# Twelve x buffers instead of eight, statistics eight node blocks ahead, and a new order of VectorE's work in a node round

## What is computed

```python
h = maximum(layernorm(x, eps=1e-5), 0)            # (100000, 160)
s, v = h[:, :64], h[:, 64:].reshape(N, 32, 3)
w = relu(edge_feature @ W_fc1) @ W_fc2            # weights of each edge
tp = products(w, (s @ W_nl0)[dst], (v @ W_nl1)[dst], unit(edge_attr))
agg = segment_sum(tp, src, N) / 32
out_s = agg[:, :96] @ W_out_s + s @ W_skip0
out_v = agg_v @ W_out_v + v @ W_skip1
fs, gate = silu(out_s[:, :64]), sigmoid(out_s[:, 64:96])
return x + concatenate([fs, gate * out_v])
```

## Time and profile before

| | |
|---|---|
| Time, three runs | 1454.20, 1448.97, 1454.13 us; median 1454.13 |
| Profiled execution: span | 1322.7 us |
| Its own device time beside the span | not listed; the median less the span is 131.4 us |
| Busy share of TensorE, VectorE, ScalarE, GpSimd | 91%, 83%, 78%, 63% |
| Edge stages, node stage | about 0 to 610 us, 610 to 1323 us |
| From the residual of block 0 to that of block 97 | 631.52 to 1314.13 us |

### The profile page before, as it was taken

One profiled execution on the slowest core, in us unless ns is written; L12 is line 12 of the kernel. 1 busy time (PEld: TensorE's weight loads), 2 busy tenths in 40 slices (PEclk: granted clock), 3 DMA queues, 4 the chain that ended last, 5 costly groups with the idle time before them and its releaser, 6 DMA issues.

```text
span 1322.7 us, 33310 instructions
## 1 busy us (share of the span) xinstructions
PE 1197.9 (91%) x8853; PEld 998.1 (75%) x8853; DVE 1099.5 (83%) x4058; ACT 1029.0 (78%) x2446; POOL 828.6 (63%) x1077
## 2 busy tenths in 40 slices
PE   4899998999999999994999998999889999889986
PEld 2455557888888888883888787888778888778876
DVE  7999998888889888875688788888788888788775
ACT  2777776788878888864888788888888887888884
POOL 5555557787878888712766566566566666566651
PEclk9999997999999999996999999999999999999998
DMA  6000002344434443422888878888878888888873
GB/s 214 8 0 0 0 15 65 105 111 111 112 104 113 112 110 108 113 60 52 218 248 245 251 225 246 248 248 253 238 231 241 253 245 248 239 235 255 241 192 108
DMA packets 90930, 212.40 MB, mean 161 GB/s; under 512 B 15030, under 2 KB 56281, under 8 KB 90878
## 3 DMA queue, kind: packets, MB, share of 16 engines
q1 hardware_dynamic: 62462, 155.23, 35.4%
q0 software_dynamic: 28416, 56.56, 21.0%
HBM read 127.73 MB, written 84.00 MB: 160 GB/s over the span
## 4 chain that ended last, share of the span: by engine, by line
PE 38%; DVE 18%; ACT 9%; issue 9%; DMA 8%; POOL 2%; SPq 0%; DVEq 0%; ACTq 0%; POOLq 0%
DMA xb<-x 7%; PE bank L1419 6%; PE bank L1349 5%; DVE n_stat L858 5%; ACT nn L1178 4%; DVE ob L949 4%; PE bank L1289 4%; PE bank L1378 3%; PE bank L1366 3%; PE bank L1433 3%; PE bank L1362 3%; PE bank L1364 3%; PE bank L1334 2%; PE bank L1411 2%; DVE ob L956 2%
## 5 line engine op out<-in xcount | busy, mean ns | idle before, releaser
L574 POOL DMA_INDIRECT mg<-messages,slot_m x392 | 430.0, 1097 | 274.5 <-issue 107.3
L1178 ACT ACTIVATE nn<-xb,n_bias,n_rstd 128x160 f32<-128x160 f32 x784 | 383.7, 650 | 91.0 <-DVE n_bias L656 91.0
L1419 PE MATMUL bank<-wsk_a,nt 128*128 128x160 f32 x1568 | 298.8, 313 | 58.3 <-DVE ob L949 57.0
L1419 PEld LDWEIGHTS bank<-wsk_a,nt 128*128 128x128 f32 x1568 | 227.2, 192 | 75.7 <-issue 57.2
L501 POOL DMA_INDIRECT xg<-x,dst_g x200 | 208.8, 1044 | 61.4 <-issue 56.1
L858 DVE BATCH_NORM_STATS2 n_stat<-xb 128x6 f32<-128x160 f32 x784 | 203.0, 314 | 29.1 <-DMA xb<-x 28.4
L949 DVE SCALAR_TENSOR_TENSOR ob<-sg,bank 128x128 f32<-128x128 f32 x588 | 131.7, 281 | 100.8 <-ACT ob L1193 100.7
L1433 PE MATMUL bank<-mg,hot 64*128 64x192 f32 x1568 | 181.8, 351 | 4.7 <-DVE hot L934 4.7
L1411 PE MATMUL bank<-ident,nn 128*128 128x128 f32 x784 | 147.8, 312 | 13.7 <-ACT nn L1178 13.7
L1185 ACT ACTIVATE nt<-bank 128x640 f32<-128x640 f32 x196 | 137.5, 702 | 23.2 <-PE bank L1412 18.5
L1411 PEld LDWEIGHTS bank<-ident,nn 128*128 128x128 f32 x784 | 110.1, 209 | 58.1 <-issue 57.4
(11 more groups left out here) (187 smaller groups left out, 2476.2 us busy)
## 6 DMA issues: line engine op xcount, KB each, us to landing
xb<-x SPq DMA_DIRECT2D x97, 640.0 KB, 6.9
out_dram<-ob SPq DMA_DIRECT2D x97, 640.0 KB, 3.6
messages<-msg SPq DMA_DIRECT2D x50, 390.6 KB
mg<-messages,slot_m POOLq DMA_INDIRECT x392
ef<-edge_feat_t SPq DMA_DIRECT2D x50, 125.0 KB, 5.9
xg<-x,dst_g POOLq DMA_INDIRECT x200
xb<-x SPq DMA_DIRECT2D x1, 420.0 KB
out_dram<-ob SPq DMA_DIRECT2D x1, 420.0 KB
```

Of the source, the lines that this page charges most:

```text
L574: pool.indirect_dma_start(mg[:, m, k, :], None, messages[:, :], bass.IndirectOffsetOnAxis(ap=slot_m[:, m, k:k + 1], axis=0)).then_inc(n.g[ ...
L1178: last = act.activation(nn[:, u % 2, h, :, g % 4], xb[:, u, g, :], ACT.Relu, bias=n_bias[:, u // U, c:c + 1], scale=n_rstd[:, u // U, c:c ...
L1419: pe.matmul(z[:, t, 0:F], nt[:, h, t * P:(t + 1) * P], wsk_a[:], start=(t % 2 == 0), stop=False, skip_group_check=True)
```

## The change

It does four things.

1. `XU` goes from 8 to 12. The loop body holds 12 rounds, and is run 6 times behind a prologue of 12 and before an epilogue of 14. SP loads twelve blocks at the start of the kernel, and block i+11 in round i. The sets of statistics go from two to three (`SETS`). The wait for a load is now counted by `turns`, a number that the loop hands on.
2. VectorE measures block i+8 in round i (before: i+6), from round 0 on (before: from round 2).
3. The extraction moves to rounds with i % 4 == 0, for blocks i+4 to i+7 (before: i+2 to i+5).
4. In a round, gate(i,0) comes right behind the masks and the seed; the statistics, with the root steps between them, come last. Before, they stood ahead of gate(i,0).

To make room in SBUF, the buffers of the binning stage are freed before `again` (a buffer of a fallback path that these inputs do not take) and those behind it are laid out.

```diff
-        U, XU = 4, 8
+        U, XU = 4, 12
+        SETS = XU // U
-        n_stat = sb("n_stat", [P, 2, U * G, 6])
+        n_stat = sb("n_stat", [P, SETS, U * G, 6])
...
-                        elif macro_exists(i + 7) and macro_exists(i - 1):
-                            load_x(i + 7, (u + 7) % XU)
+                        elif macro_exists(i + XU - 1) and macro_exists(i - 1):
+                            load_x(i + XU - 1, (u + XU - 1) % XU)
...
-                            dve.wait_ge(n.x[u], earlier(i, u, XU, 16) + 16)
+                            dve.wait_ge(n.x[u], 16 * turns + 16)
...
-                        wait(dve, n.norm, 2 * (i - U))
+                        wait(dve, n.norm, 2 * (i - (XU - U)))
...
-                        j, w = i + 2, (u + 2) % XU
-                        extract = u % U == 2 and macro_exists(j)
-                        s, v = i + 6, (u + 6) % XU
-                        measure = macro_exists(s) and macro_exists(i - 2)
+                        j, w = i + 4, (u + 4) % XU
+                        extract = u % U == 0 and macro_exists(j)
+                        s, v = i + 8, (u + 8) % XU
+                        measure = macro_exists(s)
+                        loads = turns + (u + 8) // XU
...
                         if extract:
                             seed(j, w)
-                            if measure:
-                                stats_n(s, v, 0, 1)
-                            root_a(j, w, 0)
...
-                            root_b(j, w, 2)
-                            root_c(j, w, 2)
-                        elif measure:
-                            stats_n(s, v)
                         gate(i, u, 0)
                         if extract:
+                            for k in range(3):
+                                root_a(j, w, k)
+                                if measure:
+                                    stats_n(s, v, 3 * k, 3 * k + 1, loads)
+                                root_b(j, w, k)
+                                if measure:
+                                    stats_n(s, v, 3 * k + 1, 3 * k + 2, loads)
+                                root_c(j, w, k)
+                                if measure and k < 2:
+                                    stats_n(s, v, 3 * k + 2, 3 * k + 3, loads)
                             shift_n(j, w)
+                        elif measure:
+                            stats_n(s, v, turns=loads)
```

## The result

The changed kernel takes 1412.3 us (median of 5, 1401.96 to 1416.9), the kernel before 1454.2 (median of 5, 1448.97 to 1462.64). The ratio is 0.9693, with a 95% interval of 0.9649 to 0.9737. I had forecast 1381 us with a range of 1374 to 1406, so the gain was foreseen and its size missed: 73 us forecast, 42 measured.

A forecast was written before the change was run, and what follows sets the result against it. The prediction took the three engines to be taking turns, with TensorE the floor at 6.24 us a round afterwards. 97 x (7.04 - 6.28) = 73.7 us less, all else 0, gave span 1249 plus 131.4, 1381 us, range 1374 to 1406.

The forecast's parts named there:

- the base that the rows give: Whole kernel: the median 1454.13 us stands in for the profiled execution's time, leaving 131.4 us around its 1322.7 us span.
- the cadence after the change: Node stage: rounds fall from 7.04 to 6.28 us, near TensorE's 6.24, saving 73.7 us over 97 rounds.
- all the slacks that I worked out: VectorE's gates in a node round: finished 2.4 us before TensorE's need, or 1.7 and 1.1 us in an extraction round.
- Extraction earlier: Node stage: n_bias ready two rounds, 12.5 us, before its first reader, so ScalarE's 3.23 us wait goes to zero.
- gate(i,0) earlier: VectorE's node round: TensorE's 51.7 us of gate waits go, while VectorE may wait 0.15 us for the silu.
- Twelve buffers: Node stage loads: 18.7 us allowed for a landing of 6.8, so VectorE's 25.9 us of waits for x go.
- Loads at the start: Kernel start: four more loads, 6.2 us of DMA, hidden behind the binning; taken as 0, or 6.2 without cover.
- Code: Node loop: the body of twelve rounds stays in instruction memory; taken as 0 cost, bounded by 16.5 us.
- DMA bound: Rival, node stage: buffers drain and loads come late, 6.5 us a round, 1402 us; chance 0.17.
- Code fetched again: Rival, node loop: instruction fetches stall VectorE at the loop's head, adding 0 to 11 us, 1381 to 1392; chance 0.09.
- Half the gain: Rival, node stage: ScalarE's wait goes, but a late silu delays the gates and skip; 6.7 us a round, 1421 us; chance 0.06.
- Slower: Rival, node stage: VectorE stands over 1.22 us a round at gate(i,0), 1481 us at 1.5; no gain or slower, chance 0.05.

The follow-up runs named there:

- e1: The kernel before and the changed kernel, both unedited, timed beside each other on one chip: 1478.6 us before, 1422.8 us changed, ratio 0.9619.
- e4_half_adds: The changed kernel with two of the four message adds in each half block left out: 1410.1 us, ratio 0.9518 to the kernel before.
- e2_new_order_8: The kernel before with only gate(i,0) moved ahead of root steps and statistics, eight buffers kept: 1488.0 us, ratio 1.0047.
- e3_buffers_only: The kernel before with only the twelve buffers and the loop of twelve rounds added: 1475.7 us against 1476.2, ratio 0.9975.
- e3_short_slack: The changed kernel with each load issued two rounds later, one round ahead of its statistics: 1425.1 us, ratio 0.9634 to the kernel before.
- e4_half_loads: The changed kernel with loads after the first twelve blocks bringing only half the partitions: 1431.7 us, ratio 0.9676 to the kernel before.
- e5_light_tensor_b: The changed kernel without three of four message adds and two of four wide skips, except in round 0: 1364.4 us, ratio 0.9258 to the kernel before.

## Why the forecast was wrong, step by step

**The step that failed first is the base that the rows give**: "The median of the runs, 1454.13, stands in for the profiled execution's own time, which isn't listed, and leaves 131.4 us around the span". Around a span lie 2 us. The other 129 us were inside the executions that were timed: the recorded profile shows one of a quicker kind, in which TensorE's completions were seen at once. Every row of rows 1 to 13 is of that kind. A gap of 9% between a span and the times was there to read before any forecast, and I booked it as a constant. In the total this cancels, since span and constant add up to the measured median; the 32 us by which the total was missed are all in the term that follows, which was read off rows of the wrong kind.

**The step that failed in the sum is the cadence after the change**, "I take 6.28 us a round, between 6.24 and the 6.31 seen", and with it the term "97 x (7.04 - 6.28) = 73.7". The cadence measured 7.10 and 7.15, with TensorE idle for half a microsecond of each round, and the gain 42 us in the first runs and 56 in those of `e1`. The step took for granted that TensorE's throughput sets the round. `e4_half_adds` shows that it does not: with half a microsecond less to do in each round TensorE stood idle instead. With completions up to 4 us late and more, all the slacks that I worked out (1.1, 1.7, 2.4 us) can be used up. That this is what holds the round is argued from the waits, and no run removes the late completions alone.

**What was right is which waits go**: no wait for `n_bias`, TensorE's wait for the gate from 59.3 to 11.0 us, none for x. What sets the round afterwards was not. The forecast has a difference of 0.76 us a round, from 7.04; in the profiles of `e1` it is 0.64 us, from 7.79 to 7.15. Both ends are off by about 0.8 us, so that their difference comes out near is in part luck.

**By parts.** Extraction earlier: right, nearly all of the gain. gate(i,0) earlier: the wait went as forecast, in `e2_new_order_8` without the rest of the change too, but it bought nothing that shows: less idle time of TensorE is not less time here. Twelve buffers: `e3_buffers_only` and `e3_short_slack` show nothing gained by them. In the rerun of before VectorE waited only 3.3 us for x in 600, so the 25.9 us belong to the quick kind, and what they were worth there no run shows. Loads at the start: the first residual came at 703 to 718 us in kernels with twelve loads ahead of it and at 710 and 711 us in those with eight, too scattered to price 6 us, so this is open. Code: 0, as I took it. The Trainium skill ("Runtime: NRT & Kernel Launch", "Instruction fetch mechanics") says that a taken branch whose target has left the instruction memory stalls on a fetch. In this trace no instruction packet came from 870 to 1290 us, so a body of twelve rounds stayed on every engine and the rule did not bite here.

**The rivals.** DMA bound: refuted by `e4_half_loads`. Code fetched again: refuted by the DMA view. Half the gain, by "the silu late, then gate(i,0), the statistics queued behind it": this is the one whose signs were seen (VectorE waiting for the silu, 88.5 us in 600), and its 1421 us lie 9 us from the 1412.3 measured. I gave it 6 in 100. I argued against it from slacks, in rows that held no late completion. Slower, the same wait taken to its end: it didn't come, but VectorE stands 88.5/82.8 = 1.07 us a round for the silus of both gates, where I had worked out 0.15 for one. The kernel before stands 142.1/75.6 = 1.88.

**What stays open** is why TensorE's completions come late in some executions and not in the recorded one. `e5_light_tensor_b` shows that they remain with fewer instructions on TensorE, and `e4_half_loads` shows the round no shorter with a fifth less DMA traffic; more is not shown. Nor is it shown what the change would gain in a quick execution, of which none of the changed kernel was seen.

## What to carry to other kernels

Hold a profile's span against the timed runs before using one row of it; here a gap of 131 us meant that it showed another kind of execution, and floors worked out from it were floors only. In a hand-ordered ring of engines look for the value that is made and needed in the same round, and move its making one round ahead; that was worth 3%, and further slack, deeper prefetch and a nicer order were worth nothing that showed here. Where completions jitter, judge slack against the longest wait seen and not against a mean. And when work is left out as a test, read the granted clock beside the time: in `e5_light_tensor_b` it was 0.76 instead of 0.96, and TensorE's busy time fell by 1.1 us a round where 2.9 had been left out.

## What the runs showed that I had not expected

In the timed kind of execution TensorE's semaphore increments come up to some 4 us and more after the recorded end of its matmuls (median of the adds 0.55 us in the changed kernel, 0.02 to 0.55 over all profiles of this kind), at irregular places, while ScalarE's and VectorE's come within 0.03 us in the changed kernel's node stage. Where two are held back they come together: increments for a transpose recorded at 1176.87 and an add recorded at 1179.20 came at 1181.24 and 1181.44. The granted clock follows: it was 1.00 from 1179 to 1182 us, in which TensorE was busy for 0.99 of 3 us, and 0.61 in the three behind, and four matmuls at 1182.10 took 0.91 us instead of 0.71.
